# Masks of an attention kernel's top-k tiles, all made on GpSimd by subtraction and minimum with zero

## The chip, the cores and the metric

The kernel runs on one core of a Trainium2 chip. The metric is the device time of one execution in microseconds (us), as the median of several runs. The engines of the core are called as in the profile: PE (TensorE matmul), PEld (TensorE weight load), DVE (VectorE), ACT (ScalarE), POOL (GpSimd) and SP (SyncE, which issues the DMAs here).

## The reference, cut to what matters

The reference is a transformer layer on x of shape (32, 256, 128) in float32: 32 batches of 256 rows. Attention has 16 heads of 8 columns. It sums a sparse part (softmax scores of which only the largest 12 of 256 in each row stay) and a linear part, mixed by a weight for each head; a projection, a residual and one selected linear layer are added.

```
scores = jnp.einsum('bhnd,bhmd->bhnm', q, k) / jnp.sqrt(jnp.float32(D))
aw = jax.nn.softmax(scores, axis=-1)
topk = max(1, int(N * TOPK_RATIO))            # 12
kth = jax.lax.top_k(aw, topk)[0][..., -1:]
mask = (aw >= kth).astype(aw.dtype)
aws = aw * mask
aws = aws / (aws.sum(-1, keepdims=True) + 1e-08)
o_s = jnp.einsum('bhnm,bhmd->bhnd', aws, v)
```

## The kernel before, in words

All engines run the same outer loop over batches (`body(it, ...)`), and in it eight **units** `u_`. A unit is two heads, and has four **tiles** of 128 rows x 256 keys (two heads times two halves of the 256 rows). That makes 32 x 8 = 256 units and 1024 tiles. The first six and the last six passes of the loop are written out, and between them a hardware loop of six passes runs four batches in each. The order on each engine is the order in which the code is written, and semaphores join the engines. `g` is the running number of a unit.

The way of one tile through the engines:

1. PE `scores` (L823) multiplies q and k into `score_ps`.
2. DVE `largest` (L539) finds the 8 largest scores of each row. POOL (L371) subtracts the second largest: `drop`.
3. ACT (L724) writes `e` = exp of the scores with `drop` as bias, four instructions for a unit, and L729 does the same for the 8 largest (`e8`).
4. DVE `remove` (L546) writes `rest`, which is `e` with its 8 largest replaced by -1, and `following` (L552) finds the next 8. Entry `TOPK - 9` of `next8` is the 12th largest of the row, which is the threshold.
5. The **mask** `below` (bf16) must be nonzero where `e` lies under the threshold and 0 elsewhere. POOL makes it (L393) with one comparison `is_lt`, which gives 1.0 or 0.0, for the first 3, 2, 3, 4, 4, 4, 3 or 2 tiles of a unit (`POOL_TILES`, by ring place `r`). ACT makes the others (L737) as Relu(threshold - e). That is 25 tiles of 32 in a batch on POOL and 7 on ACT.
6. PE `turn` (L841 and L842) transposes `e` into `turn_ps` and adds to it the transposed mask, by a matmul with `minus_huge`, a diagonal of -2^40. ACT (L694) copies it with a Relu into `kept`, which clears what lay under the threshold.
7. PE `product` (L862) multiplies `kept` with v. Once a batch, `sums` (L873), DVE L586 to L594, and PE L901 to L915 make the output, which ACT copies (L770) and SP stores.

Rings: `score_ps`, `top`, `drop` and `e8` have 2 places; `e`, `next8` and `below` have 8 (`RING`); `kept` has 4.

The distances between the engines are written into the bodies. In the body of unit g, DVE takes `largest` of g and then `remove` and `following` of g - 1. POOL takes `drop` of g and then the masks of g - 2. ACT takes `kept` of g - 4, `e` of g, and its masks of g - 2. PE takes `turn` of g - 4 and then `scores` of g + 1. POOL also does other work on 128x512 or smaller tiles, once a batch (L336 to L358, L381, L401, L409 to L429: the layer norms of x, q and k, and the linear attention's sums). PE waits in `turn` for all four masks of its unit, by two semaphores, `below_pool` and `below_act`.

Of the kernel before, what the change touches and what calls it, by code (L numbers as in the profile page):

```python
# [57 lines left out]
POOL_TILES = (3, 2, 3, 4, 4, 4, 3, 2)  # L58
POOL_SUM = sum(POOL_TILES)
POOL_UPTO = tuple(sum(POOL_TILES[:v]) for v in range(UNITS + 1))  # L60
# [10 lines left out]
def wait(engine, semaphore, value):  # L71

    if isinstance(value, int) and value <= 0:
        return None
    return engine.wait_ge(semaphore, value)  # L75
# [9 lines left out]
def build(nc, x, Wqkv, bqkv, q_gamma, q_beta, k_gamma, k_beta, alpha, Wproj, bproj, W, bW, logits, u, y):  # L85
# [12 lines left out]
    def exists(batch):  # L98
        return not isinstance(batch, int) or 0 <= batch < B

    with ExitStack() as ctx:
        def sb(name, shape, dt=F32):
            return ctx.enter_context(nc.sbuf_tensor(name, shape, dt))
# [4 lines left out]
        def sem(name):  # L108
# [4 lines left out]
        minus_huge = sb("minus_huge", [P, P], BF16)  # L113
# [93 lines left out]
            exp_done below_pool below_act turn_ready turn_copied pv_ready pv_copied  # L207
# [82 lines left out]
        def _(pool):  # L290
# [6 lines left out]
            nc.gpsimd.memset(minus_huge[:], 0.0).then_inc(s["pool_step"], 1)  # L297
# [4 lines left out]
            select(minus_huge[:], ALU.not_equal, -HUGE, 0, [[-1, P]], 1, 4).then_inc(s["pool_const"], 1)  # L302
# [59 lines left out]
            def body(it, par, xr):  # L362
                nxt = 1 - par
                for u_ in range(UNITS):
# [23 lines left out]
                    if exists(it if u_ >= 2 else it - 1):  # L388

                        r = (u_ - 2) % RING  # L390
                        for t in range(POOL_TILES[r]):
                            wait_alone(pool, s["next_ready"], TILES * (g - 2) + t + 1, s["waits_passed"])
                            nc.gpsimd.tensor_scalar(below[:, r, t, :], e[:, r, t, :],  # L393
                                                    next8[:, r, t, TOPK - 9:TOPK - 8], None,
                                                    ALU.is_lt).then_inc(s["below_pool"], 1)
# [254 lines left out]
        def _(act):  # L650
# [32 lines left out]
            def body(it, par, xr):  # L683
                nxt = 1 - par
                for u_ in range(UNITS):
# [45 lines left out]
                    if exists(it if u_ >= 2 else it - 1):  # L731

                        r = (u_ - 2) % RING
                        act.wait_ge(s["next_ready"], TILES * (g - 1))
                        for t in range(POOL_TILES[r], TILES):

                            nc.scalar.activation(below[:, r, t, :], e[:, r, t, :], ACT.Relu, scale=-1.0,  # L737
                                                 bias=next8[:, r, t, TOPK - 9:TOPK - 8]).then_inc(s["below_act"], 1)


# [56 lines left out]
        def _(pe):  # L797
# [8 lines left out]
            def body(it, par, xr):  # L806
# [20 lines left out]
                def turn(u_):  # L827

                    g2 = it * UNITS + u_ - 4
                    r = (u_ - 4) % RING  # L830
                    batch = it if u_ >= 4 else it - 1
                    pe.wait_ge(s["below_pool"], POOL_SUM * batch + POOL_UPTO[r + 1])
                    wait(pe, s["below_act"], (UNITS * TILES - POOL_SUM) * batch + TILES * (r + 1) - POOL_UPTO[r + 1])
                    wait(pe, s["turn_copied"], g2)
                    for hh in range(2):
                        for nt in range(NT):
                            t = 2 * hh + nt
                            for mc in range(NT):
                                dst = turn_ps[:, hh, mc, nt * P:(nt + 1) * P]
                                keys = slice(mc * P, (mc + 1) * P)  # L840
                                mm(dst, e[:, r, t, keys], ident[:], start=True, stop=False, is_transpose=True)  # L841
                                last = mm(dst, below[:, r, t, keys], minus_huge[:], start=False, stop=True)  # L842
                    last.then_inc(s["turn_ready"], 1)
# [175 lines left out]
```

## Time and profile before

| what | us |
|---|---|
| median of 3 runs | 1256.25 (1255.8, 1256.25, 1259.92) |
| the profiled execution, its own time | 1254.07 |
| its span in the trace | 1252.3 |
| DVE busy | 1187.9 (95%) |
| ACT busy | 1086.6 (87%) |
| POOL busy | 1083.9 (87%) |
| PE busy | 972.0 (78%) |

Busy time is the time in which an engine has an instruction in work. A share of the whole span mixes the start, in which the engines wait for one another, the long middle, and the end, in which one batch runs out. So the engines are read stretch by stretch, and the waits beside them.

### The profile page before, as it was taken

How to read it: one execution, taken by the hardware profiler on the slowest of the kernel's cores; microseconds unless marked ns; L12 is line 12 of the kernel's file. 1: busy time of each engine (PE TensorE's matmuls, PEld its weight loads, DVE VectorE, ACT ScalarE, POOL GpSimd, SP SyncE). 2: the span in 40 equal slices, each digit the busy share in tenths (PEclk: the TensorE clock that was granted, in tenths of full speed). 3: DMA queues.
4: the chain of work that ended last, by engine and by line, in shares of the span. 5: the costliest groups of instructions: out<-in, count | busy, mean ns of one | idle time of the engine just before them, and what ended most of it. 6: DMA issues, size and time to landing. Idle time of an engine off the chain costs nothing.

```text
span 1252.3 us, 38772 instructions
## 1 busy us (share of the span) xinstructions
PE 972.0 (78%) x8997; PEld 655.4 (52%) x9028; DVE 1187.9 (95%) x4553; ACT 1086.6 (87%) x3626; POOL 1083.9 (87%) x1688
## 2 busy tenths in 40 slices
PE   2578788887788777877877888788868788877876
PEld 0245555555455554555545555455545555555554
DVE  7699999999899998999989999899989999999994
ACT  2498999999799997999979899799988999999984
POOL 4598999999899997999979999799988999999974
PEclk9999999899899998999989999899999998999998
DMA  2122221212221222221122221122221222222110
GB/s 61 47 73 78 81 80 40 70 57 82 83 82 43 66 69 72 82 81 54 55 59 82 82 81 51 48 69 82 82 84 36 67 63 82 81 81 71 41 52 14
DMA packets 165211, 83.45 MB, mean 67 GB/s; under 512 B 7753, under 2 KB 164943, under 8 KB 164946
## 3 DMA queue, kind: packets, MB, share of 16 engines
q1 hardware_dynamic: 164946, 80.56, 22.4%
q8 instruction: 88, 1.44, 0.5%
q14 instruction: 177, 1.45, 0.4%
HBM read 42.78 MB, written 37.75 MB: 64 GB/s over the span
## 4 chain that ended last, share of the span: by engine, by line
DVE 53%; issue 32%; DVEq 6%; PE 5%; POOL 2%; ACT 1%; SPq 0%; DMA 0%; POOLq 0%; ACTq 0%
DVE rest L546 22%; DVE top L539 18%; DVE next L552 8%; DVEq L75 5%; POOL below L393 2%; PE turn_ps L841 1%; PE pv_ps L862 1%; DVE o_sparse L594 1%; DVE lin_z L567 1%; PE turn_ps L842 1%; ACT e L724 1%; DVE stats L602 0%; DVE den L586 0%; DVE x_mv L608 0%; DVE lin L570 0%
## 5 line engine op out<-in xcount | busy, mean ns | idle before, releaser
L393 POOL TENSOR_SCALAR below<-e,next 128x256 bf16<-128x256 f32 x800 | 724.6, 922 | 0.2 <-issue 0.2
L724 ACT ACTIVATE e<-score_ps,drop 128x256 f32<-128x256 f32 x1024 | 473.2, 481 | 53.8 <-POOL drop L371 51.3
L841 PE MATMUL turn_ps<-ident,e 128*128 128x128 f32 x2048 | 406.5, 292 | 61.9 <-issue 22.4
L546 DVE MATCH_REPLACE8 rest<-e 128x256 f32<-128x256 f32 x1024 | 409.8, 402 | 0.0
L552 DVE MAX8 next<-rest 128x8 f32<-128x256 f32 x1024 | 402.9, 406 | 0.0
L539 DVE MAX8 top<-score_ps 128x8 f32<-128x256 f32 x1024 | 358.8, 408 | 31.5 <-issue 16.9
L842 PE MATMUL turn_ps<-minus_huge,below 128*128 128x128 bf16 x2048 | 383.9, 226 | 0.0
L841 PEld LDWEIGHTS turn_ps<-ident,e 128*128 128x128 f32 x2048 | 300.3, 147 | 107.2 <-issue 62.2
L694 ACT ACTIVATE kept<-turn_ps 128x1024 f32<-128x1024 f32 x256 | 267.6, 1045 | 68.1 <-PE turn_ps L842 67.8
L842 PEld LDWEIGHTS turn_ps<-minus_huge,below 128*128 128x128 bf16 x2048 | 224.9, 110 | 0.2
L724 ACT ACTIVATION_READ_ACCUMULATOR e<-score_ps,drop 128x1 f32 x1024 | 217.6, 213 | 0.0
L862 PE MATMUL pv_ps<-kept,v_aug 128*32 128x256 f32 x2048 | 145.5, 404 | 1.9 <-ACT out_sb L770 1.3
L371 POOL TENSOR_TENSOR drop<-top 128x36 f32<-128x36 f32 x256 | 62.8, 245 | 82.3 <-DVE top L539 81.7
L823 PE MATMUL score_ps<-k_slots,q_slots 64*128 64x256 bf16 x1024 | 104.7, 282 | 19.4 <-ACT e L724 11.1
L737 ACT ACTIVATE below<-e,next 128x256 bf16<-128x256 f32 x224 | 108.2, 516 | 0.0
L862 PEld LDWEIGHTS pv_ps<-kept,v_aug 128*32 128x32 f32 x2048 | 55.6, 113 | 49.5 <-issue 29.5
L823 PEld LDWEIGHTS score_ps<-k_slots,q_slots 64*128 64x128 bf16 x1024 | 31.0, 95 | 79.8 <-issue 72.8
L939 PE MATMUL work_ps<-w_qk,xnT 128*128 128x256 f32 x128 | 46.8, 448 | 31.6 <-ACT xnT L786 31.6
L546 DVE MATCH_VALUE_LOAD rest<-e 128x8 f32 x1024 | 68.4, 67 | 0.8 <-ACT e L729 0.8
L729 ACT ACTIVATE e<-drop 128x32 f32<-128x32 f32 x256 | 63.4, 248 | 0.0
L873 PE MATMUL pv_ps<-gather,oT 128*128 128x128 f32 x256 | 35.0, 280 | 29.4 <-ACT oT L746 29.2
L958 PE MATMUL work_ps<-kv,qfT 128*128 128x144 f32 x128 | 25.3, 322 | 35.1 <-DVE kv L560 35.1
(156 smaller groups left out, 1333.0 us busy)
## 6 DMA issues: line engine op xcount, KB each, us to landing
part_slots<-part SPq DMA_DIRECT2D x128, 192.0 KB, 2.3
q_slots<-part_slots SPq DMA_DIRECT2D x64, 256.0 KB, 3.4
k_slots<-part_slots SPq DMA_DIRECT2D x64, 256.0 KB, 4.0
part_slots<-part SPq DMA_DIRECT2D x64, 128.0 KB, 2.0
x_sb<-in_L_attn_x SPq DMA_DIRECT2D x32, 128.0 KB, 4.0
x_res<-in_L_attn_x SPq DMA_DIRECT2D x32, 128.0 KB, 3.9
out_y<-out_sb SPq DMA_DIRECT2D x32, 128.0 KB, 4.4
w_ops<-in_L_ffn_W SPq DMA_DIRECT2D x1, 512.0 KB
```

What stands on the lines that cost most here:

```text
L393: nc.gpsimd.tensor_scalar(below[:, r, t, :], e[:, r, t, :], next8[:, r, t, TOPK - 9:TOPK - 8], None, ALU.is_lt).then_inc(s["below_pool"], 1)
L539: nc.vector.max(top[:, q, t, 1:9], score_ps[:, q, t // 2, t % 2, :]).then_inc(s["top_ready"], 1)
L546: nc.vector.match_replace(rest[:, t, :], e8[:, (u_ - 1) % 2, t, :], e[:, (u_ - 1) % RING, t, :], REMOVED).then_inc(s["rest_ready"], 1)
L552: nc.vector.max(next8[:, (u_ - 1) % RING, t, :], rest[:, t, :]).then_inc(s["next_ready"], 1)
L694: nc.scalar.activation(kept[:, u_ % 4], turn_ps[:], ACT.Relu).then_inc(s["turn_copied"], 1)
L724: nc.scalar.activation(e[:, u_ % RING, t, :], score_ps[:, u_ % 2, t // 2, t % 2, :], ACT.Exp, bias=drop[:, u_ % 2, t, 0:1], accum_out=z[:, ...
L729: nc.scalar.activation(e8[:, u_ % 2], drop[:, u_ % 2, :, 1:9], ACT.Exp).then_inc(s["e8_ready"], 1)
L737: nc.scalar.activation(below[:, r, t, :], e[:, r, t, :], ACT.Relu, scale=-1.0, bias=next8[:, r, t, TOPK - 9:TOPK - 8]).then_inc(s["below_a ...
L823: last = mm(score_ps[:, v_ % 2, hh, nt, :], q_slots[rows, side, v_, nt * P:(nt + 1) * P], k_slots[rows, side, v_, :], start=True, stop=True)
L841: mm(dst, e[:, r, t, keys], ident[:], start=True, stop=False, is_transpose=True)
L842: last = mm(dst, below[:, r, t, keys], minus_huge[:], start=False, stop=True)
L862: last = mm(pv_ps[32 * j:32 * (j + 1), 0:N], v_aug[:, side, mc, 4 * q + j, :], kept[:, v_ % 4, j % 2, mc, :], start=(mc == 0), stop=(mc == ...
```

## The change

The mask of every tile is made by POOL. In place of the comparison stands one instruction with two operations: `e` minus the threshold, and then the minimum of that and 0.0. Under the threshold the mask is now a negative number (the distance), elsewhere it is 0. The diagonal matrix changes its sign with it and is called `huge`. ACT makes no masks any more, and the wait in ACT for `next_ready` goes with them. PE waits for one semaphore, `below_ready`, which counts four masks for each unit. The ring sizes, the distances between the engines and everything else stay.

```diff
-POOL_TILES = (3, 2, 3, 4, 4, 4, 3, 2)
-POOL_SUM = sum(POOL_TILES)
-POOL_UPTO = tuple(sum(POOL_TILES[:v]) for v in range(UNITS + 1))
...
-            select(minus_huge[:], ALU.not_equal, -HUGE, 0, [[-1, P]], 1, 4).then_inc(s["pool_const"], 1)
+            select(huge[:], ALU.not_equal, HUGE, 0, [[-1, P]], 1, 4).then_inc(s["pool_const"], 1)
...
                         r = (u_ - 2) % RING
-                        for t in range(POOL_TILES[r]):
+                        for t in range(TILES):
                             wait_alone(pool, s["next_ready"], TILES * (g - 2) + t + 1, s["waits_passed"])
                             nc.gpsimd.tensor_scalar(below[:, r, t, :], e[:, r, t, :],
-                                                    next8[:, r, t, TOPK - 9:TOPK - 8], None,
-                                                    ALU.is_lt).then_inc(s["below_pool"], 1)
+                                                    next8[:, r, t, TOPK - 9:TOPK - 8], 0.0,
+                                                    ALU.subtract, ALU.min).then_inc(s["below_ready"], 1)
...
-                    if exists(it if u_ >= 2 else it - 1):
-
-                        r = (u_ - 2) % RING
-                        act.wait_ge(s["next_ready"], TILES * (g - 1))
-                        for t in range(POOL_TILES[r], TILES):
-
-                            nc.scalar.activation(below[:, r, t, :], e[:, r, t, :], ACT.Relu, scale=-1.0,
-                                                 bias=next8[:, r, t, TOPK - 9:TOPK - 8]).then_inc(s["below_act"], 1)
...
-                    batch = it if u_ >= 4 else it - 1
-                    pe.wait_ge(s["below_pool"], POOL_SUM * batch + POOL_UPTO[r + 1])
-                    wait(pe, s["below_act"], (UNITS * TILES - POOL_SUM) * batch + TILES * (r + 1) - POOL_UPTO[r + 1])
+                    pe.wait_ge(s["below_ready"], TILES * (g2 + 1))
...
-                                last = mm(dst, below[:, r, t, keys], minus_huge[:], start=False, stop=True)
+                                last = mm(dst, below[:, r, t, keys], huge[:], start=False, stop=True)
```

Three lines go at the head of the file, so the lines of GpSimd's part lie three lower in the changed kernel (L393 becomes L390).

The first place is POOL in the middle of a batch, units 1 to 3. Before:

```order
L371 TENSOR_TENSOR drop<-top 128x36
L393 TENSOR_SCALAR below<-e,next 128x256 x2
L336 TENSOR_TENSOR qk_rsqrt<-qk_rsqrt 128x64
L338 TENSOR_SCALAR qk_rsqrt<-qk_rsqrt 128x64
L340 TENSOR_TENSOR qk_rsqrt<-qk_rsqrt 128x64
L349 TENSOR_TENSOR qk_a<-qk_raw,qk_rsqrt 128x512
L371 TENSOR_TENSOR drop<-top 128x36
L358 TENSOR_TENSOR qk_b<-qk_a,gamma 128x512
L393 TENSOR_SCALAR below<-e,next 128x256 x3
L371 TENSOR_TENSOR drop<-top 128x36
```

The same place in the changed kernel:

```order
L368 TENSOR_TENSOR drop<-top 128x36
L390 TENSOR_SCALAR below<-e,next 128x256 x4
L333 TENSOR_TENSOR qk_rsqrt<-qk_rsqrt 128x64
L335 TENSOR_SCALAR qk_rsqrt<-qk_rsqrt 128x64
L337 TENSOR_TENSOR qk_rsqrt<-qk_rsqrt 128x64
L346 TENSOR_TENSOR qk_a<-qk_raw,qk_rsqrt 128x512
L368 TENSOR_TENSOR drop<-top 128x36
L355 TENSOR_TENSOR qk_b<-qk_a,gamma 128x512
L390 TENSOR_SCALAR below<-e,next 128x256 x4
L368 TENSOR_TENSOR drop<-top 128x36
```

Between two `drop` instructions there are now four masks where there were two or three; the order is otherwise the same.

The second place is ACT near the end of the program, in two of the last batch's units. Before:

```order
L724 ACTIVATE e,z<-score_ps,drop 128x256 x4
L729 ACTIVATE e<-drop 128x32
L737 ACTIVATE below<-e,next 128x256 x2
L694 ACTIVATE kept<-turn_ps 128x1024
L724 ACTIVATE e,z<-score_ps,drop 128x256 x4
L729 ACTIVATE e<-drop 128x32
L737 ACTIVATE below<-e,next 128x256
L746 COPY oT<-pv_ps 128x256
```

The same place in the changed kernel:

```order
L721 ACTIVATE e,z<-score_ps,drop 128x256 x4
L726 ACTIVATE e<-drop 128x32
L691 ACTIVATE kept<-turn_ps 128x1024
L721 ACTIVATE e,z<-score_ps,drop 128x256 x4
L726 ACTIVATE e<-drop 128x32
L733 COPY oT<-pv_ps 128x256
```

The masks are gone from ACT's order, and nothing takes their place there.

## Rows read from the trace of the kernel before

**Rows 1.** The page: busy us, share of the span, number of instructions

```profile
PE 972.0 (78%) x8997; PEld 655.4 (52%) x9028; DVE 1187.9 (95%) x4553; ACT 1086.6 (87%) x3626; POOL 1083.9 (87%) x1688
```

**Rows 2.** Busy time by stretch: from:to and length, each engine's busy us, PE clock, DMA

```profile
0.00:53.30 53.30, 18.37 (x58) 8.76 (x59) 33.16 (x120) 18.16 (x66) 22.21 (x59) 1.00 0.22 63
53.30:1236.00 1182.70, 942.91 (x8844) 639.06 (x8874) 1153.80 (x4432) 1064.28 (x3554) 1061.68 (x1630) 0.96 0.23 67
1236.00:1252.30 16.30, 10.73 (x100) 7.63 (x98) 0.97 (x3) 4.18 (x8) 0.00 (x0) 1.00 0.09 25
...
500.00:600.00 100.00, 80.89 (x785) 55.23 (x788) 99.86 (x384) 92.93 (x310) 92.20 (x143) 1.00 0.27 77
```

**Rows 3.** Waits of DVE: line waited for, us in total, times, longest

```profile
DVE top L539 <- issue: 16.9, 5, 3.6
DVE top L539 <- PE score_ps L823: 13.6, 8, 5.7
...
DVE rest L546 <- ACT e L729: 0.8, 1, 0.8
```

**Rows 4.** The page's groups of masks: busy us, mean ns, idle before them

```profile
L393 POOL TENSOR_SCALAR below<-e,next 128x256 bf16<-128x256 f32 x800 | 724.6, 922 | 0.2 <-issue 0.2
...
L737 ACT ACTIVATE below<-e,next 128x256 bf16<-128x256 f32 x224 | 108.2, 516 | 0.0
```

**Rows 5.** POOL's groups by shape, the nearest to the new instruction

```profile
L381 POOL TENSOR_TENSOR sq_half<-qk_sq 128x256 f32<-128x256 f32 x32 | 23.4, 730 | 6.6 <-ACT qk_sq L789 6.6
...
L338 POOL TENSOR_SCALAR qk_rsqrt<-qk_rsqrt 128x64 f32<-128x64 f32 x32 | 7.9, 247 | 6.4 <-POOL qk_rsqrt L336 6.4
...
L338 POOL TENSOR_SCALAR x_rsqrt<-x_rsqrt 128x2 f32<-128x2 f32 x32 | 6.1, 191 | 6.4 <-POOL x_rsqrt L336 6.4
...
L293 POOL TENSOR_SCALAR_AFFINE_SELECT ident<-ident 128x128 f32<-128x128 f32 x1 | 0.3, 292 | 0.2 <-POOL ident L295 0.2
L293 POOL TENSOR_SCALAR_AFFINE_SELECT minus_huge<-minus_huge 128x128 bf16<-128x128 bf16 x1 | 0.3, 292 | 0.1
```

**Rows 6.** POOL's timeline at a loop boundary: start, us, line, count, idle before

```profile
330.49 3.61 POOL L393 TENSOR_SCALAR below<-e,next 128x256 bf16<-128x256 f32 x4
334.06 0.63 POOL L429 TENSOR_TENSOR k_feat<-k_exp,k_rec 128x256 f32<-128x256 f32 x1
337.87 0.24 POOL L371 TENSOR_TENSOR drop<-top 128x36 f32<-128x36 f32 x1 [3.17 <-DVE top L539]
```

**Rows 7.** POOL's waits

```profile
POOL drop L371 <- DVE top L539: 81.7, 120, 6.6
```

**Rows 8.** POOL's timeline at the end of the program

```profile
1223.60 3.61 POOL L393 TENSOR_SCALAR below<-e,next 128x256 bf16<-128x256 f32 x4
1227.58 0.24 POOL L371 TENSOR_TENSOR drop<-top 128x36 f32<-128x36 f32 x1 [0.37 <-DVE top L539]
1227.80 8.10 POOL L393 TENSOR_SCALAR below<-e,next 128x256 bf16<-128x256 f32 x9
```

**Rows 9.** PE's timeline: the first transposition of each of the last four units

```profile
1227.27 0.48 PE L841 MATMUL turn_ps<-ident,e 128*128 128x128 f32 x1 [3.26 <-POOL below L393]
...
1231.88 0.48 PE L841 MATMUL turn_ps<-ident,e 128*128 128x128 f32 x1
...
1235.40 0.30 PE L841 MATMUL turn_ps<-ident,e 128*128 128x128 f32 x1 [0.82 <-ACT kept L694]
...
1238.21 0.30 PE L841 MATMUL turn_ps<-ident,e 128*128 128x128 f32 x1 [0.26 <-ACT kept L694]
```

**Rows 10.** DVE's timeline: the last two groups of `following`, units 254 and 255

```profile
1229.51 0.74 DVE L552 MAX8 next<-rest 128x8 f32<-128x256 f32 x2
...
1232.39 0.74 DVE L552 MAX8 next<-rest 128x8 f32<-128x256 f32 x2
```

More of the change, by code:

```diff
@@ L112, in build @@
         ident = sb("ident", [P, P])
-        minus_huge = sb("minus_huge", [P, P], BF16)
+        huge = sb("huge", [P, P], BF16)
         minus_one = sb("minus_one", [P, P], BF16)
@@ L206, in build @@
             scores_ready top_ready rest_ready next_ready drop_ready e8_ready waits_passed
-            exp_done below_pool below_act turn_ready turn_copied pv_ready pv_copied
+            exp_done below_ready turn_ready turn_copied pv_ready pv_copied
             x_stats x_mean x_rsqrt_step x_rsqrt_ready x_newton xn_ready
@@ L296, in _ @@
             select(ident[:], ALU.not_equal, 1.0, 0, [[-1, P]], 1, 1).then_inc(s["ident_ready"], 1)
-            nc.gpsimd.memset(minus_huge[:], 0.0).then_inc(s["pool_step"], 1)
+            nc.gpsimd.memset(huge[:], 0.0).then_inc(s["pool_step"], 1)
             nc.gpsimd.memset(own_head[:], 1.0).then_inc(s["pool_step"], 1)
```

## The prediction, made before the changed kernel ran

> **What bounds the kernel now.** I read the busy shares first [rows 1]: DVE has 95% of the span, ACT and POOL 87% each. Since these are means over unlike stretches, the windows come next [rows 2]. From 500 to 600 us, inside the loop, DVE is busy 99.86 us of 100, POOL 92.20, ACT 92.93 and PE 80.89. The reader is to see that DVE has no gap there at all, and that POOL has only 8% in hand. In the stretch in which masks are made (53.3 to 1236.0 us, 1182.7 us long) DVE is busy 1153.80 us, so 28.9 us are idle. The waits of DVE tell whose they are [rows 3]: 16.9 us are "issue" before L539, five times up to 3.6 us, at the turns of the hardware loop; 13.6 us are waits for PE's scores, eight times, one of 5.7 us. ACT kept DVE waiting for 0.8 us in all. No row has DVE wait for a mask, because a mask goes to PE's `turn` and has two units of slack. So the masks are off the path that sets the time, in the whole program but its end. There the last masks are followed by transpositions, products and the output, and POOL is late [rows 8, 9].
>
> **What the change takes away.** 224 mask instructions of 516 ns on ACT, 108.2 us busy [rows 4]. ACT is not the bound (it has 1064.28 us in the stretch of 1182.7 us [rows 2]) and DVE hardly waits for it [rows 3], so I count this as nothing: DVE's own 1153.80 us cover it, and ACT, with more room, triggers nothing that DVE takes time for. The wait of ACT for `next_ready` goes too. It was met before ACT came to it, for a row of L737 has no idle time before it [rows 4].
>
> **What it adds.** 224 more masks on POOL. Everything hangs on the price of one mask there, since POOL has little in hand. So I first work out which price is the turning point. In the stretch from 53.3 to 1236.0 us POOL is busy 1061.68 us [rows 2]; 724.6 us of these are its 800 masks [rows 4], which leaves 337 us of other work. I estimate 54 us of idle time that POOL can't shed: 5 loop turns of about 3.2 us, as the one before `drop` at 337.87 us [rows 6], make 16 us; the short gaps between chained small instructions make the rest, about 38 us, of which the two groups of L338 show 6.4 us each [rows 5]. If DVE goes on setting the length of the stretch, 1182.7 - 337 - 54 = 792 us are left for 1024 masks: **0.77 us each**, from start to start. Below that the kernel stays as it is, above it POOL becomes the bound.
>
> **The price of the new instruction.** No row shows subtraction and minimum on POOL. The bounds:
> - From below: the one other two-operation instruction with a scalar is L338 (multiply, then add). It takes 191 ns at 2 elements a partition and 247 ns at 64 [rows 5]. That is 56 ns for 62 elements, or 0.90 ns for one, and at 256 elements 191 + 254 x 0.90 = **420 ns**.
> - In the middle: the two-tensor addition L381 has the same shape, 128x256, and 730 ns [rows 5]. It has to fetch two tensors where the mask has one.
> - From above: the comparison of now, 922 ns [rows 4]. By the same base of 191 ns it costs (922 - 191) / 254 = 2.9 ns for an element, over three times as much as L338. If each operation of the new instruction cost what the comparison costs, it would be 191 + 2 x 731 = **1653 ns**.
>
> What makes the comparison so dear decides between them. It differs from L338 in three things: it yields a truth value that must be made into 1.0 or 0.0, it writes bf16 from float32, and its scalar comes from memory. The second can be tested a little: the selection over 128x128 takes 292 ns in bf16 as in float32 [rows 5]. So the type alone costs POOL nothing there, although no row shows a change of type. For the third I know no row; but one scalar in a partition is read once, and could hardly cost 2 ns for each of 256 elements. That leaves the first, which the change takes away. So I take the lower end, 420 ns, and keep all up to 1653 ns for the rivals. The same L338 shows that two operations need not cost two passes.
>
> The page "GPSIMD Engine Reference" of the Trainium skill has a rule on this (section 3.1): loops with at most two operations on an element run at 1.03 cycles for each, bound by the port; its section 7 gives 2.03 cycles for loops that compare and select, unless they are unrolled twice. At its 1.2 GHz 1.03 cycles are 0.86 ns, beside the 0.90 ns of L338 [rows 5]; the comparison's 2.9 ns here is more than the page has for either. By the page the new mask would be some 410 ns by estimate, and the sum would be the same; if the comparison's price were the page's 2.03 cycles and no more, there would be nothing like as much to gain on POOL.
>
> **The middle at 420 ns.** 1024 x 0.42 = 430 us of masks in place of 724.6 us. POOL then has 337 + 430 = 767 us of work in the stretch of 1182.7 us, or 65%. DVE stays at its 1153.80 us, and its idle 28.9 us are loop turns and waits for PE, in which no mask takes part: change 0. The same holds up to the 0.77 us worked out above, L381's 730 ns among it.
>
> **The end at 420 ns.** Here masks are on the path. POOL makes the masks of unit 252 from 1223.60 to 1227.21 us, then `drop` of unit 255 at 1227.58 and the last nine from 1227.80 to 1235.90 us [rows 8]. PE stood waiting for unit 252's, 3.26 us long, and began at 1227.27 us [rows 9]. With 0.41 us from start to start:
> - unit 252: masks done at 1223.60 + 4 x 0.41 = 1225.2 us, `turn` from 1225.3 us, 1.9 us earlier;
> - unit 253: masks done at 1227.80 + 1.6 = 1229.4 us, `turn` from 1229.5 us in place of 1231.88 us, 2.4 us earlier;
> - unit 254: `turn` began 3.52 us after the one of 253 [rows 9], bound by PE's own work and ACT's copy. Kept at that, it begins at 1233.0 us; its masks are done long before, since the last `following` of the unit ends at 1230.25 us [rows 10];
> - unit 255: 2.81 us later [rows 9], at 1235.9 us in place of 1238.21 us. The last `following` ends at 1233.13 us [rows 10], the mask at 1233.6 us, so it is not the bound.
>
> So the end comes **2.3 us** earlier. What follows (the last product, the sums, the output, until 1252.3 us) is unchanged. The bounds: not more than 1238.21 - 1233.6 = 4.6 us, where `turn` of 255 follows its masks at once; not less than 0, where the gaps before 1225.3 and 1229.5 us leave TensorE at its lower clock for longer. Its slow and fast transpositions of the same shape stand side by side there, 0.48 and 0.30 us [rows 9].
>
> **The sum.** The profiled execution took 1254.07 us, with a span of 1252.3 us. Less 2.3 us it is 1251.8 us. The median of the three runs, 1256.25 us, lies 2.2 us above the profiled one; against it the forecast is 1256.25 - 2.3 = **1254.0 us**, or 0.2% less. A measurement of this kernel tells about 0.3% (3.8 us) from no change, so this counts as the same.
>
> **Rivals.**
> 1. *POOL becomes the bound, at the old price* (slower). This is the one on the other side. If the dear part of the comparison is the bf16 output, the scalar from memory or the way POOL treats any operation outside multiply and add, the new mask costs about what the old one did, 0.906 us from start to start (724.6 / 800 [rows 4]). Then POOL needs 337 + 1024 x 0.906 + 54 = 1319 us in the stretch, and with 53.3 us before and 16.3 us behind the span is 1389 us, 136 us more: **about 1392 us**. It decides from 0.77 us a mask. Place: POOL's queue. `drop` stands behind the four masks there, so ACT's `e` and then DVE's L546 come late by what POOL lacks. For it speaks that every mask has the same 922 ns, whatever DVE does, so the price is POOL's own; against it the 0.90 ns of L338. A second mechanism would end in the same place: the minimum has to wait for the subtraction's result on each element, and a loop that doesn't take several elements at once pays that wait each time. But L338 adds to the result of its multiplication in the same way, at 0.90 ns. The Trainium skill gives a price for such a wait ("GPSIMD Engine Reference", section 7: a float32 chain in which each step needs the one before costs 4 cycles for each element unless it is unrolled). That is 3.3 ns by estimate, a mask of about 1040 ns, and by it the sum would be some 1500 us; no row here shows that price.
> 2. *Two dear operations* (much slower): 1.64 us from start to start. The stretch is 337 + 1679 + 54 = 2070 us, the time **about 2140 us**. L338 speaks against it.
> 3. *A larger gain* (faster): POOL's queue delivers `drop` without masks in its way. POOL waits for DVE 81.7 us in 120 of 256 cases [rows 7], so in the other 136 `drop` was late by something. If that also eased the waits behind the loop turns (a part of DVE's 13.6 us for scores [rows 3]) and the end gave the full 4.6 us, the time would be **about 1248 us**. Against it: DVE waited for ACT's `e` only 0.8 us in all, so an earlier `drop` finds nobody waiting; the waits for scores stand behind PE, which comes late from the loop turn.
>
> **How the numbers follow.** The cheap mask with a gain at the end of 0 to 4.6 us: 0.72, with its likeliest value 1254.0 us. The larger gain: 0.10. POOL bound at the old price: 0.12. Two dear operations or a price between: 0.06. The first two hold 0.82, so the range need not reach the slow ones: from 1248 us (rival 3) to 1261 us (no gain, on a run as slow as the slowest of before, 1259.92 us, rounded up). The first case can itself end a little over 3.8 us below, or above it by spread: I give faster 0.15, same 0.66, slower 0.19, where nearly all of slower are rivals 1 and 2.
>
> **What would show it.** POOL's mask group: 1024 instructions with a mean near 420 ns, POOL busy 1083.9 - 724.6 + 430 = near 790 us, ACT near 978 us, DVE unchanged at 1188 us and again 99.9% busy inside the loop. At the end, `turn` of unit 252 within 2 us of the scores before it. Wrong it would be if the mean of a mask lay above 770 ns: then POOL has 99% in the windows inside the loop and DVE waits for ACT's `e`, which waits for `drop`. A mean between 420 and 770 ns would leave the time and take from the gain at the end.

## The result, and the profile after

The changed kernel took 1599.48 us in the median (1595.93 to 1601.53), the kernel before 1256.03 us on the same chip: a ratio of 1.273, with a 95% interval of 1.269 to 1.277. The forecast was 1254.0 us, no measurable change, with a range up to 1261 us. The kernel came out 27% slower. That is the mechanism of rival 1, at a price above the one it named.

The page of the changed kernel: its span, and the busy time of each engine (the line that answers to [rows 1]).

```profile
span 1598.0 us, 38626 instructions
...
PE 1146.3 (72%) x8997; PEld 748.8 (47%) x9028; DVE 1221.7 (76%) x4553; ACT 1010.5 (63%) x3402; POOL 1503.1 (94%) x1912
```

DVE issues the same 4553 instructions, in a span 346 us longer. POOL is the full engine now: on the chain that ended last it has 62% of the span, where DVE had 53% before. The busy time by stretch, to be laid beside [rows 2], shows the same: inside the loop (the first line below) POOL is busy 97.45 us of 100, and DVE 77.33 where it had 99.86. The second line is nearly the whole program.

```profile
500.00:600.00 100.00, 74.13 (x585) 49.20 (x586) 77.33 (x291) 66.58 (x224) 97.45 (x123) 0.83 0.20 57
53.30:1590.00 1536.70, 1123.83 (x8922) 736.97 (x8952) 1187.86 (x4434) 991.52 (x3335) 1481.05 (x1853) 0.83 0.18 52
```

The group of masks on the page answers to [rows 4]; ACT's group is gone. Under it stand the two groups of multiply-add that the price was taken from (they answer to [rows 5]), and one of a single multiplication:

```profile
L390 POOL TENSOR_SCALAR below<-e,next 128x256 bf16<-128x256 f32 x1024 | 1151.0, 1146 | 1.7 <-DVE next L549 1.7
...
L335 POOL TENSOR_SCALAR qk_rsqrt<-qk_rsqrt 128x64 f32<-128x64 f32 x32 | 7.9, 248 | 6.4 <-POOL qk_rsqrt L333 6.4
...
L409 POOL TENSOR_SCALAR x_shift<-x_shift 128x2 f32<-128x2 f32 x32 | 7.5, 234 | 6.4 <-POOL x_shift L406 6.4
...
L335 POOL TENSOR_SCALAR x_rsqrt<-x_rsqrt 128x2 f32<-128x2 f32 x32 | 6.1, 192 | 6.4 <-POOL x_rsqrt L333 6.4
```

A mask takes 1146 ns, not 420. The two multiply-adds cost what they did (248 and 192 ns, against 247 and 191). DVE's busy time is 34 us higher with the same instructions; no run asks why. The waits show the chain back from POOL (engine, line, what it waited for: us, times, longest). They answer to [rows 3, 7]:

```profile
ACT e L721 <- POOL drop L368: 403.4, 237, 4.0
DVE rest L543 <- ACT e L726: 190.7, 170, 2.4
...
PEld turn_ps L826 <- POOL below L390: 89.1, 89, 3.3
```

`drop` stands behind four masks in POOL's queue and comes late, ACT waits for it 403.4 us with `e`, and DVE waits 190.7 us for ACT where it had waited 0.8 us. TensorE waits more too, and its mean granted clock is 0.83 of the full one from 500 to 600 us, where it had been 1.00.

### The profile page after: what moved, and what is told of

The parts are those of the page before. It is cut to its first block, busy times and chain, and to the rows that moved or that the text cites. A ratio compares the mean times of both kernels' runs of the same rounds, so it can differ in the third digit from the quotient of the medians.

```text
span 1598.0 us, 38626 instructions
## 1 busy us (share of the span) xinstructions
PE 1146.3 (72%) x8997; PEld 748.8 (47%) x9028; DVE 1221.7 (76%) x4553; ACT 1010.5 (63%) x3402; POOL 1503.1 (94%) x1912
## 4 chain that ended last, share of the span: by engine, by line
POOL 62%; issue 23%; DVE 5%; PE 4%; POOLq 3%; ACT 1%; DVEq 0%; SPq 0%; DMA 0%; ACTq 0%
POOL below L390 47%; POOLq L72 3%; POOL drop L368 2%; POOL qkn L355 2%; POOL d_sub L398 2%; DVE top L536 1%; DVE rest L543 1%; POOL sq_half L378 1%; ACT e L721 1%; PE turn_ps L826 1%; POOL k_half L419 1%; POOL k_feat L426 1%; PE work_ps L924 1%; PE pv_ps L847 1%; POOL sq_quarter L378 1%
## 5 line engine op out<-in xcount | busy, mean ns | idle before, releaser
L390 POOL TENSOR_SCALAR below<-e,next 128x256 bf16<-128x256 f32 x1024 | 1151.0, 1146 | 1.7 <-DVE next L549 1.7
L721 ACT ACTIVATE e<-score_ps,drop 128x256 f32<-128x256 f32 x1024 | 471.7, 473 | 407.1 <-POOL drop L368 403.4
L826 PE MATMUL turn_ps<-ident,e 128*128 128x128 f32 x2048 | 483.4, 328 | 101.9 <-POOL below L390 83.5
L827 PE MATMUL turn_ps<-huge,below 128*128 128x128 bf16 x2048 | 453.2, 249 | 0.0
L826 PEld LDWEIGHTS turn_ps<-ident,e 128*128 128x128 f32 x2048 | 344.4, 168 | 176.6 <-POOL below L390 89.1
L827 PEld LDWEIGHTS turn_ps<-huge,below 128*128 128x128 bf16 x2048 | 250.0, 122 | 0.8
L543 DVE MATCH_VALUE_LOAD rest<-e 128x8 f32 x1024 | 78.4, 77 | 191.3 <-ACT e L726 190.7
L847 PE MATMUL pv_ps<-kept,v_aug 128*32 128x256 f32 x2048 | 166.7, 452 | 1.2 <-ACT out_sb L757 1.2
L897 PE MATMUL pv_ps<-x_res,ident 128*128 128x128 f32 x128 | 34.8, 363 | 92.0 <-issue 91.5
L924 PE MATMUL work_ps<-w_qk,xnT 128*128 128x256 f32 x128 | 60.8, 567 | 43.6 <-ACT xnT L773 41.9
L368 POOL TENSOR_TENSOR drop<-top 128x36 f32<-128x36 f32 x256 | 64.0, 250 | 16.3 <-DVE top L536 16.1
L912 PE MATMUL work_ps<-w_v,xnT 128*128 128x128 f32 x128 | 32.8, 340 | 57.1 <-ACT part L745 57.1
L897 PEld LDWEIGHTS pv_ps<-x_res,ident 128*128 128x128 f32 x128 | 25.2, 245 | 98.8 <-issue 98.1
L953 PE MATMUL work_ps<-ident,qkn 128*128 128x128 f32 x128 | 33.0, 408 | 46.1 <-POOL qkn L355 46.1
```

The source lines that it names most:

```text
L368: nc.gpsimd.tensor_tensor(drop[:, q], top[:, q], top[:, q, :, 1:2].to_broadcast([P, TILES, 9]), ALU.subtract).then_inc(s["drop_ready"], 1)
L390: nc.gpsimd.tensor_scalar(below[:, r, t, :], e[:, r, t, :], next8[:, r, t, TOPK - 9:TOPK - 8], 0.0, ALU.subtract, ALU.min).then_inc(s["bel ...
L543: nc.vector.match_replace(rest[:, t, :], e8[:, (u_ - 1) % 2, t, :], e[:, (u_ - 1) % RING, t, :], REMOVED).then_inc(s["rest_ready"], 1)
L721: nc.scalar.activation(e[:, u_ % RING, t, :], score_ps[:, u_ % 2, t // 2, t % 2, :], ACT.Exp, bias=drop[:, u_ % 2, t, 0:1], accum_out=z[:, ...
L827: last = mm(dst, below[:, r, t, keys], huge[:], start=False, stop=True)
L847: last = mm(pv_ps[32 * j:32 * (j + 1), 0:N], v_aug[:, side, mc, 4 * q + j, :], kept[:, v_ % 4, j % 2, mc, :], start=(mc == 0), stop=(mc == ...
```

## What the experiments were to tell apart

The theory after the result has two parts. First, POOL's queue sets the time, and its length is the sum of its instructions; moving the masks costs nothing else. Second, the new instruction has its own high price. The rivals are that the move itself (the order on ACT, the one semaphore, the crowding on POOL) costs part of it, and that the price comes of something else in the instruction than its operations.

## The prices, measured by themselves

`price_list` is the kernel before, with groups of four POOL instructions put behind its last mask. Each group differs in one thing. `ts` is `nc.gpsimd.tensor_scalar`, `F` and `Bf` are float32 and bf16 tiles, `thr` is a scalar in memory, and the line numbers are those of the rows.

```diff
             iterations(pool, body)
+            group(lambda i: ts(Bf(i), src, thr, None, ALU.is_lt))                  # L456
...
+            group(lambda i: ts(Bf(i), src, 0.25, None, ALU.is_lt))                 # L458
...
+            group(lambda i: ts(Bf(i), src, thr, 0.0, ALU.subtract, ALU.min))       # L460
+            group(lambda i: ts(F(i), src, thr, 0.0, ALU.subtract, ALU.min))        # L461
+            group(lambda i: ts(F(i), src, 0.25, 0.0, ALU.subtract, ALU.min))       # L462
...
+            group(lambda i: ts(F(i), src, 2.0, None, ALU.mult))                    # L466
+            group(lambda i: ts(F(i), src, 2.0, 1.0, ALU.mult, ALU.add))            # L467
+            group(lambda i: ts(Bf(i), src, 2.0, 1.0, ALU.mult, ALU.add))           # L468
+            group(lambda i: ts(F(i), src, thr, 1.0, ALU.mult, ALU.add))            # L469
```

> The kernel before, with 21 groups of four GpSimd instructions behind its last mask, which write to tiles of their own; their results go nowhere. Each group changes one thing against the mask: the scalar (from memory or a constant), the output type (bf16 or float32), the operations, the size. The kernel's own part should take what it took (1256 us), plus some 70 us of prices. Known: comparison with a scalar from memory to bf16 922 ns, subtraction and minimum in that form 1144 ns. Theory A (the scalar from memory is the dear part): with a constant the comparison and the subtraction with minimum fall to about 420 to 500 ns, and multiply-add with a scalar from memory rises to over 900 ns. Theory B (the bf16 output is dear): every float32 form is near 420 ns, multiply-add to bf16 is over 900 ns. Theory C (operations other than multiply and add are dear): subtraction alone or minimum alone in float32 with a constant stay near 900 ns, multiply-add at 256 elements is 420 ns. Theory D (the line through 2 and 64 elements was no measure of 256 elements, and all forms have one loop whose price depends on the number of operations): multiply-add at 256 elements itself is far from 420 ns.

The run was made once, and only the prices are read from it. The groups by shape (busy us, mean ns | idle before):

```profile
L471 POOL TENSOR_SCALAR pr_f<-pr_src,pr_thr 128x512 f32<-128x512 f32 x4 | 7.9, 1997 | 0.1
L460 POOL TENSOR_SCALAR pr_b<-pr_src,pr_thr 128x256 bf16<-128x256 f32 x4 | 4.5, 1146 | 0.1
L461 POOL TENSOR_SCALAR pr_f<-pr_src,pr_thr 128x256 f32<-128x256 f32 x4 | 4.5, 1143 | 0.1
L462 POOL TENSOR_SCALAR pr_f<-pr_src 128x256 f32<-128x256 f32 x4 | 4.2, 1067 | 0.1
...
L456 POOL TENSOR_SCALAR pr_b<-pr_src,pr_thr 128x256 bf16<-128x256 f32 x4 | 3.6, 925 | 0.1
...
L466 POOL TENSOR_SCALAR pr_f<-pr_src 128x256 f32<-128x256 f32 x4 | 3.3, 855 | 0.1
...
L458 POOL TENSOR_SCALAR pr_b<-pr_src 128x256 bf16<-128x256 f32 x4 | 3.3, 849 | 0.1
...
L470 POOL TENSOR_SCALAR pr_f<-pr_src,pr_thr 128x64 f32<-128x64 f32 x4 | 1.9, 503 | 0.1
L469 POOL TENSOR_SCALAR pr_f<-pr_src,pr_thr 128x256 f32<-128x256 f32 x4 | 1.9, 483 | 0.1
...
L468 POOL TENSOR_SCALAR pr_b<-pr_src 128x256 bf16<-128x256 f32 x4 | 1.5, 409 | 0.1
L467 POOL TENSOR_SCALAR pr_f<-pr_src 128x256 f32<-128x256 f32 x4 | 1.5, 407 | 0.1
```

L470 and L471 are subtraction and minimum at 64 and 512 elements. In the form of the masks the prices are those of the kernels: 1146 ns here and in the changed kernel, 925 ns for the comparison against 922 [rows 4]. So a mask costs the same by itself as in the full kernel. Four readings:

- The bf16 output is free: 1146 against 1143 ns, 409 against 407. Theory B falls.
- The scalar from memory adds 76 ns to one instruction and no more: 925 against 849, 1143 against 1067, 483 against 407. Theory A falls.
- Multiply-add at 256 elements takes 407 ns. The line drawn through 2 and 64 elements in the prediction gave 420, so theory D falls: the line was right.
- A multiplication **alone** takes 855 ns, twice as much as multiplication and addition together. So the comparison was not dear for being a comparison. Theory C is right in that multiply-add is the exception, and wrong in naming the kind of operation: a multiplication alone is slow too.

`price_list_2`, also made once, has other pairs in the same place, to see how wide the exception is.

```diff
+            group(lambda i: ts(F(i), src, 2.0, 0.0, ALU.mult, ALU.subtract))       # L456
+            group(lambda i: ts(F(i), src, 2.0, 3.0, ALU.add, ALU.mult))            # L457
+            group(lambda i: ts(F(i), src, 2.0, 3.0, ALU.subtract, ALU.mult))       # L458
+            group(lambda i: ts(F(i), src, 2.0, 3.0, ALU.mult, ALU.mult))           # L459
+            group(lambda i: ts(F(i), src, 2.0, 3.0, ALU.add, ALU.add))             # L460
...
+            group(lambda i: ts(F(i), src, 2.0, 3.0, ALU.max, ALU.min))             # L464
...
+            group(lambda i: ts(F(i, 512), pr_src[:], thr, None, ALU.is_lt))        # L468
```

> As price_list, with 18 other groups of GpSimd instructions behind the last mask; their results go nowhere. Known by now: multiply-add 407 ns, with a scalar from memory 483, every single operation 850 to 855 with a constant, subtraction and minimum 1067 with a constant and 1143 with a scalar from memory. Theory E (one special loop for multiply-add alone, and a general one for all else that takes operations in turn): every other pair, also add-multiply, multiply-multiply and add-add, costs about 1067 ns. Theory F (a fast loop for all pairs of add, subtract and multiply, and a slow one once minimum, maximum or a comparison is in the pair): those pairs are near 407 ns, and only pairs with minimum, maximum or is_lt near 1067. Theory G (only the second operation decides): multiply-subtract and subtract-multiply differ. The comparison at 64 and 512 elements gives the slope of one operation: near 2.5 ns an element if the second operation costs 0.85 ns of the 3.3 that subtraction and minimum show.

```profile
L468 POOL TENSOR_SCALAR pr_f<-pr_src,pr_thr 128x512 f32<-128x512 f32 x4 | 6.2, 1563 | 0.1
...
L456 POOL TENSOR_SCALAR pr_f<-pr_src 128x256 f32<-128x256 f32 x4 | 4.2, 1082 | 0.1
...
L460 POOL TENSOR_SCALAR pr_f<-pr_src 128x256 f32<-128x256 f32 x4 | 4.2, 1073 | 0.1
L458 POOL TENSOR_SCALAR pr_f<-pr_src 128x256 f32<-128x256 f32 x4 | 4.2, 1074 | 0.1
...
L464 POOL TENSOR_SCALAR pr_f<-pr_src 128x256 f32<-128x256 f32 x4 | 4.2, 1064 | 0.1
...
L469 POOL TENSOR_SCALAR pr_f<-pr_src 128x512 f32<-128x512 f32 x4 | 2.4, 620 | 0.1
...
L459 POOL TENSOR_SCALAR pr_f<-pr_src 128x256 f32<-128x256 f32 x4 | 1.5, 408 | 0.1
L457 POOL TENSOR_SCALAR pr_f<-pr_src 128x256 f32<-128x256 f32 x4 | 1.5, 406 | 0.1
L470 POOL TENSOR_SCALAR pr_f<-pr_src,pr_thr 128x2 f32<-128x2 f32 x4 | 1.1, 304 | 0.1
L471 POOL TENSOR_SCALAR pr_f<-pr_src,pr_thr 128x2 f32<-128x2 f32 x4 | 1.1, 291 | 0.1
```

L469 is multiply-add over 512 elements; L470 is subtraction and minimum, and L471 the comparison, over 2.

Only three of the pairs tried are fast: multiply-add, add-multiply and multiply-multiply, 406 to 408 ns. Every other pair, add-add and multiply-subtract among them, takes 1064 to 1082 ns with constants. Theory E is nearly right, with three pairs in place of one; F and G fall. In the other form, here called the general one, an element costs (1563 - 925) / 256 = 2.5 ns with one operation, and (1997 - 1143) / 256 = 3.3 ns with two. An instruction of it over 2 elements costs some 300 ns with the scalar from memory (L470, L471), where multiply-add with constants has 191 [rows 5]. Why POOL treats these three pairs otherwise no run shows.

## The sum of POOL's queue, tested from three sides

**The prediction's own sum, with its price made true.** The mask's two operations become multiply and add (the kernel then leaves out the top-k selection).

```diff
                                                     next8[:, r, t, TOPK - 9:TOPK - 8], 0.0,
-                                                    ALU.subtract, ALU.min).then_inc(s["below_ready"], 1)
+                                                    ALU.mult, ALU.add).then_inc(s["below_ready"], 1)
```

> The changed kernel with the two operations of the mask replaced by multiply and add (same scalar from memory, same constant, same tiles and types). The masks then hold no top-k selection: that part of the computation is left out, and every instruction stays. It has the price that the prediction assumed, 483 ns measured in price_list against 420. By the prediction's sum GpSimd is no longer the bound, the middle takes what it took before, the end comes 2.3 us earlier: 1254 us. Rival (moving ACT's masks to GpSimd costs something besides GpSimd's time): it stays above 1262 us. Rival (a freer GpSimd gives more, since drop comes sooner): 1248 us or less.

It took 1255.07 us, and its ratio to the kernel before is 0.999, interval 0.997 to 1.001. So the whole move (all masks on POOL, none on ACT, one semaphore) costs nothing where the mask is cheap. The page and the window inside the loop:

```profile
PE 982.3 (78%) x9028; PEld 666.6 (53%) x9028; DVE 1187.9 (95%) x4553; ACT 1002.4 (80%) x3402; POOL 838.2 (67%) x1912
...
500.00:600.00 100.00, 83.05 (x778) 57.03 (x776) 99.86 (x384) 85.61 (x292) 70.52 (x160) 0.97 0.27 77
```

DVE is busy 99.86 us of 100 as before, and POOL 70.52. Rival 3 is answered too. POOL now makes `drop` as soon as DVE's maxima are there (it waits for them 323.9 us), ACT is busy 84 us less, and DVE gains nothing. The prediction had 978 us for ACT, which is busy 1002.4: it took off the 108.2 us of the masks' group, but instructions on ACT overlap in the trace, and its groups add up to more than its busy time.

**The operation undone, the move kept.** The changed kernel with the comparison of before:

```diff
-                                                    next8[:, r, t, TOPK - 9:TOPK - 8], 0.0,
-                                                    ALU.subtract, ALU.min).then_inc(s["below_ready"], 1)
+                                                    next8[:, r, t, TOPK - 9:TOPK - 8], None,
+                                                    ALU.is_lt).then_inc(s["below_ready"], 1)
```

> The changed kernel with the one operation undone: all 1024 masks on GpSimd, but by the comparison of before, with the diagonal of -2^40. If the sum of GpSimd's queue is right (337 us other work, 54 us it can't shed, 0.906 us for a mask from start to start, 53.3 and 16.3 us around it), the span is 1389 us and the time about 1391 us, with GpSimd busy near 97% inside the loop. Rival: the sharing out is harmless and the dear operation alone makes the loss; then it stays near 1256 us. Rival: something else in the move, as the order on ACT or the single semaphore, costs most of it; then it is far above 1391 us, near 1600 us.

It took 1389.96 us, ratio 1.107 (1.104 to 1.111), with a span of 1387.7 us where the sum said 1389. **The operation changed, the move undone:** the kernel before, with subtraction and minimum on POOL's 25 tiles.

```diff
-                                                    next8[:, r, t, TOPK - 9:TOPK - 8], None,
-                                                    ALU.is_lt).then_inc(s["below_pool"], 1)
+                                                    next8[:, r, t, TOPK - 9:TOPK - 8], 0.0,
+                                                    ALU.subtract, ALU.min).then_inc(s["below_pool"], 1)
...
-                                last = mm(dst, below[:, r, t, keys], minus_huge[:], start=False, stop=True)
+                                last = mm(dst, below[:, r, t, keys], (huge if t < POOL_TILES[r] else minus_huge)[:], start=False, stop=True)
```

> The kernel before with the operation alone changed: GpSimd makes its 25 of 32 masks by subtraction and minimum, ACT keeps its 7, and PE uses a diagonal of the sign that fits the tile. By the sum with 1.124 us from start to start (800 masks, 899 us): 337 + 899 + 54 + 70 = 1360 us of span, time about 1362 us, GpSimd bound. Rival: the price per mask of 1144 ns in the changed kernel came of its crowding (masks that wait for one another); then it falls back to about 922 ns here and the time stays at 1256 us.

PE is given a diagonal of the sign that fits the tile. It took 1356.69 us, ratio 1.081 (1.076 to 1.086), 5 us under the sum. Its masks took 1145 ns each, so the price is no matter of crowding. The two halves of the change therefore cost about 134 us (the move at the old price) and about 101 us (the dearer operation at the old share). Together they cost 343 us, 109 more than the two added up. Of that, 49 us are the 224 moved masks at the dearer price (224 x 0.22). The rest is the room that POOL had beside DVE, which the sum puts at 792 - 725 = 67 us: each half alone uses it up, and the two together can use it only once. 49 + 67 = 116 us, against the 109 measured.

**Where POOL stops being the bound.** The same kernel with 22, and then 20, of 32 masks on POOL.

```diff
-POOL_TILES = (3, 2, 3, 4, 4, 4, 3, 2)
+POOL_TILES = (2, 2, 2, 4, 4, 3, 3, 2)
```

> As submin_25, with GpSimd making 22 of 32 masks and ACT 10. The sum for GpSimd is 337 + 704 x 1.124 + 54 = 1182 us in the stretch of masks, just what DVE needs there; ACT gets 96 masks more, 46 us, which leaves it some 70 us under the stretch. So the time should be 1256 to 1275 us: the turning point lies here. Rival: the engines are so chained that ACT's added work, or GpSimd at 97%, already costs more; then it is above 1290 us.

> As submin_22, with 20 of 32 masks on GpSimd by subtraction and minimum and 12 on ACT. In submin_22 GpSimd's batch is 37.1 us long from drop to drop, without gaps, and DVE's own batch is 36.1 us; two masks less are 2.25 us less, 34.9 us. Theory (GpSimd was still the bound at 22): the time falls back to 1256 to 1265 us. Rival (ACT is what costs now, with 12 masks): it stays at or above 1308 us.

With 22 it took 1308.17 us (ratio 1.042, 1.038 to 1.046), 33 us above the end of what was expected. With 20, shared out as (3, 2, 2, 3, 3, 3, 2, 2), it took 1266.60 us (ratio 1.0075, 1.005 to 1.010), 2 us above the end of what was expected. The sum was short by something at 22. From 500 to 600 us of submin_22 neither engine was full:

```profile
500.00:600.00 100.00, 78.45 (x700) 53.19 (x700) 91.63 (x351) 86.22 (x292) 89.18 (x122) 0.91 0.20 57
```

POOL has 89.18 us and DVE 91.63 (the fifth and third busy times), so each has times in which it waits. The timeline of POOL's `drop` in submin_22 suggested why. One unit has four masks (4.50 us) and the sums of k beside them, and the next `drop` comes 5.80 us after the one before, where DVE needs some 4.5 us for a unit (1153.80 us [rows 2] over 256 units):

```profile
215.04 0.24 POOL L374 TENSOR_TENSOR drop<-top 128x36 f32<-128x36 f32 x1 [0.20 <-DVE top L542]
215.27 4.50 POOL L396 TENSOR_SCALAR below<-e,next 128x256 bf16<-128x256 f32 x4
...
220.84 0.24 POOL L374 TENSOR_TENSOR drop<-top 128x36 f32<-128x36 f32 x1
```

So the same 22 masks were shared out by what else POOL has in each unit, which kept the total:

```diff
-POOL_TILES = (2, 2, 2, 4, 4, 3, 3, 2)
+POOL_TILES = (3, 2, 3, 3, 4, 3, 2, 2)
```

> As submin_22, with the same 22 of 32 masks on GpSimd in a batch, but shared out by what else GpSimd has in each unit: (3, 2, 3, 3, 4, 3, 2, 2) by ring place in place of (2, 2, 2, 4, 4, 3, 3, 2). submin_22 took 1308 us where the sum said 1256 to 1275. Theory (unevenness: a unit with four masks and the sums of k beside them keeps drop back by more than the slack of one unit, and DVE does not get it back): the time falls to 1265 to 1285 us. Rival (the total of GpSimd's batch decides, 37.1 us against DVE's 36.1): it stays at 1300 us or above.

It took 1270.17 us, ratio 1.014 (1.011 to 1.017). Of the 52 us that submin_22 lost, some 35 us (by the two ratios) were its uneven sharing and not its total. From 200 to 320 us the distance from `drop` to `drop` goes from 3.7 to 5.8 us in submin_22, and from 4.0 to 5.1 us here. The loss did not reach DVE mainly through `e`: in submin_22 DVE waited 10.2 us for `e`, 26.5 us for PE's scores and 31.1 us for PE's sums, and here 3.9, 17.7 and 11.7 us. The steps between are not traced. Its window shows both engines near full:

```profile
500.00:600.00 100.00, 81.17 (x775) 55.60 (x777) 99.81 (x385) 94.66 (x316) 95.56 (x134) 0.98 0.22 62
```

## Two more tests of which engine sets the time

Both kernels leave out the maximum of each head's 8 columns (DVE) and its subtraction (POOL) ahead of the exponentials in the linear part. The softmax is the same without them.

```diff
-                        pool.wait_ge(s["dmax_ready"], it + 2)
-                        nc.gpsimd.tensor_tensor(heads(d_sub[:]), heads(qkn[:]), spread(d_max[:]),
-                                                ALU.subtract).then_inc(s["dsub_ready"], 1)
...
-                        nc.vector.tensor_reduce(d_max[:], qkn[:].rearrange("p (g d) -> p g d", d=D), AX_X,
-                                                ALU.max).then_inc(s["dmax_ready"], 1)
...
-                        act.wait_ge(s["dsub_ready"], it + 2)
-                        sub = d_sub[:].rearrange("p (t a c) -> p t a c", t=NT, a=2)
+                        act.wait_ge(s["qkn_ready"], it + 2)
+                        sub = qkn[:].rearrange("p (t a c) -> p t a c", t=NT, a=2)
```

Made in the changed kernel:

> The changed kernel without the maximum of each head's 8 columns on DVE (L575, about 21 us) and its subtraction on GpSimd (L398, 34.7 us busy and 8.9 us of waiting before it); the softmax is the same without them. If GpSimd alone sets the time of the changed kernel, what comes off is its own 43.6 us, and DVE's 21 us count for nothing: 1599.5 - 43.6 = 1556 us. If DVE were on the path too, up to 21 us more come off, 1535 us; if the two engines' waits for each other were the bound, it is less than 20 us.

It took 1555.23 us, 44 us less than the changed kernel's 1599.48: POOL's own 43.6 us. DVE's 21 us counted for nothing.

Made in the kernel before:

> The kernel before, with its own masks, without the maximum of each head's 8 columns (DVE L578, 21.1 us) and its subtraction (GpSimd L401, 34.5 us) ahead of the exponentials of q and k in the linear part; a softmax is the same without them. If DVE sets the time wherever it is 99.9% busy, all of its 21 us come off: about 1235 us. Rival (the others are as near to the bound): less than 8 us comes off.

It took 1239.37 us, ratio 0.988 (0.984 to 0.991): by the ratio 16 us less, most of DVE's 21. Its profiled execution had a span of 1233.4 us, 18.9 us under the one of before. Here DVE's microseconds count. The subtraction that POOL loses as well can hardly be the reason, since mask_muladd freed far more of POOL and gained nothing. This version is faster than both kernels; it has nothing to do with the masks.

## Why the prediction was wrong, point by point

- **What bounds the kernel before** was right: DVE, with no mask on its path, and POOL with 8% in hand. mask_muladd and no_max bear it out.
- **The turning point**, 0.77 us a mask, lay a little too high. With 22 of 32 masks at 1.124 us POOL has as much to do in masks as with 1024 of 0.77 us, and that came to 1.4% over the kernel before, once evenly shared, and 4.2% as first shared. The prediction counted totals only, and near the turning point the sharing out among units counts as well.
- **The price of the new instruction** is the step that failed. The prediction took 420 ns from L338 and measured was 1146. The number for L338's pair was right (407 ns at 256 elements). The error is the sentence that laid the comparison's high price on its being a comparison and then gave subtraction and minimum the price of multiply and add. The only fast instruction in view was itself the exception. One POOL row of the kernel before that the prediction left unread spoke against it. The single multiplication over 128x2 takes 235 ns there (the median is 227), and multiply-add over the same shape 191 ns [rows 5]:

```profile
L412 POOL TENSOR_SCALAR x_shift<-x_shift 128x2 f32<-128x2 f32 x32 | 7.5, 235 | 6.4 <-POOL x_shift L409 6.4
```

One operation dearer than two says that the two have a form of their own. The same base of 191 ns was also put under the comparison, which has 291 ns over 2 elements; so its price for an element came out as 2.9 ns, and it is (925 - 291) / 254 = 2.5. The two other readings of the comparison held: neither the output type nor the scalar from memory (76 ns) makes it dear.
- **The upper end** was 1653 ns, from taking the comparison's price twice. The bounds of the price held the true one, though the range of the time did not; but a whole second pass isn't paid: the second operation adds 218 ns (1067 - 849), some 0.85 ns for each element.
- **The sum at a given price** was right. At 0.906 us it gave 1389 us of span and cmp_all had 1387.7. At the 1.124 us of the changed kernel (1151.0 / 1024) it gives 53.3 + 337 + 1151 + 54 + 16.3 = 1612 us, and the span was 1598.0. In that trace POOL's last mask ends at 1581.2 us, so the stretch of masks has 1527.9 us. POOL is busy 1481.05 of them, 330 us besides the masks, and idle 47: the two terms of 337 and 54 us were 7 us too long each. The share in the windows was 97%, not the 99% that the prediction named as the sign.
- **The rule of the Trainium skill.** "GPSIMD Engine Reference" gives 1.03 cycles for each element in loops with at most two operations (section 3.1). The multiply-add agrees: 1.03 cycles at the page's 1.2 GHz are 0.86 ns, and (620 - 407) / 256 is 0.83 ns. The general form doesn't, at 2.5 and 3.3 ns, and the new mask, some 410 ns by that rule, took 1146. The page's price of 4 cycles for a float32 chain (section 7), told beside rival 1, is 3.3 ns by estimate, the very slope of two general operations. Whether a chain is the cause no run here shows, and single operations cost 2.5 ns too. It gave some 1500 us, the nearest figure in the prediction; what it lacked is mostly the base, which was taken as 191 ns and is 304 (L470 of price_list_2).
- **The end of the program** was wrong as well, by little. It should have given 2.3 us back with a cheap mask; in mask_muladd the span is 1252.7 us, against 1252.3. The wait of PE for unit 252's masks [rows 9] had a second cause right behind the first. Before its transposition PE also waits until ACT has copied unit 251 (the semaphore `turn_copied`). That copy, in the kernel before, ran until 1226.90 us; the masks ended at 1227.21:

```profile
1225.84 1.06 ACT L694 ACTIVATE kept<-turn_ps 128x1024 f32<-128x1024 f32 x1
```

In mask_muladd the same unit's masks were done at 1226.11 us, and PE waited all the same until 1227.69, now for the copy:

```profile
1226.50 1.05 ACT L691 ACTIVATE kept<-turn_ps 128x1024 f32<-128x1024 f32 x1
...
1227.69 0.45 PE L826 MATMUL turn_ps<-ident,e 128*128 128x128 f32 x1 [3.19 <-ACT kept L691]
```

DVE's last `largest` starts 0.65 us later in this run (1226.62 us, against 1225.97), so against DVE the transposition came 0.2 us earlier, not 1.9. For unit 253 the prediction looked at the masks alone as well. PE makes its transpositions of unit 252 and the products of the pair of units before it first, and unit 253's began 4.61 us after unit 252's before and 4.60 us after it in mask_muladd (1227.69 to 1232.29). The 2.4 us put down to the masks there were PE's own work.

- **The chances.** The slow cases had 0.18 together. The 0.90 ns of L338 was one row of one pair of operations, and the bounds of the price lay on both sides of the turning point. That should have kept far more weight on the slow side, and the range open to it.

## What to carry to other kernels

A price measured for one pair of operations on GpSimd says nothing of another pair; time the exact instruction at the exact size before an engine with 8% in hand gets 28% more of it. Work out the price at which the engine becomes the bound first, since that sum was good to 1% where POOL was clearly the bound (cmp_all, submin_25, the changed kernel), and spend the effort on the price. Near the turning point it was less good: submin_22 came out 33 us above what was expected. Where two engines are both near full, what a unit of work holds in each step counts as well as the total: the same 22 masks took 1308 or 1270 us. And before a wait is counted as gain, look at what the waiting instruction waits for next.

## What the runs showed that was not expected

- On GpSimd a multiplication alone (855 ns over 128x256 in float32) takes twice the time of multiplication and addition in one instruction (407 ns). Subtraction of a broadcast tensor, as a two-tensor instruction, takes 615 ns and so beats subtraction of a scalar, 851 ns with a constant and 927 ns from memory.
- The output type made no difference (1146 against 1143 ns, 409 against 407), and a scalar from memory costs 76 ns an instruction.
- An idle engine is no use to the bound: mask_muladd freed 246 us of POOL's time and 84 us of ACT's, and the kernel took what it took before.
